# Attention inside a transformer block on eight cores: the probability-times-V matmuls run two groups behind the scores instead of one

## The reference

```python
xn = _layernorm(x, axis=-1)
x = x + attn(xn) + ffn(xn)

# attn
q, k, v = xn@Wq + bq, xn@Wk + bk, xn@Wv + bv
scores = jnp.einsum('bqhk,bshk->bhqs', q, k) * scale
attn = jax.nn.softmax(scores, axis=-1)
ctx = jnp.einsum('bhqs,bshk->bqhk', attn, v)
y = x + jnp.einsum('bqhk,hkd->bqd', ctx, Wo) + bo      # then layernorm, gamma, beta

# ffn: softmax router, top 2 of 8 experts, renormalized
hidden = jax.nn.silu(gate_out) * up_out
expert_out = jnp.einsum('enf,efd->end', hidden, down_w)
```

## Time and profile before

| what | us |
|---|---|
| the three runs | 7039.46, 7514.11, 7524.77 |
| their median | 7514.11 |
| the profiled execution's own time | 7039.46 |
| its span, first to last instruction, slowest core (core 3) | 7037.9 |
| spans of the eight cores | 7002.6 to 7037.9 |
| mean granted TensorE clock of the cores, as a share of 2.4 GHz | 0.788 to 0.791 |

### The profile page before, as it was taken

The page is one execution under the profiler, slowest core; times in us unless marked ns, Lnnn a source line. Parts: engine busy times, 40 slices in busy tenths (PEclk is TensorE's granted clock), DMA queues, the critical chain, the costliest instruction groups (busy, mean ns, idle before and its releaser), DMA issues.

```text
span 7037.9 us, 122186 instructions; the slowest of 8 cores (7002.6 to 7037.9 us)
## 1 busy us (share of the span) xinstructions
PE 5573.7 (79%) x49824; PEld 3157.8 (45%) x49824; DVE 2016.0 (29%) x3908; ACT 2595.2 (37%) x2802; POOL 57.4 (1%) x112
## 2 busy tenths in 40 slices
PE   2577777777777777777777337999999989999999
PEld 1355555555555555555555113444444434444444
DVE  3423232332323233233332563212212211212121
ACT  0266666566666666666666001111111111111111
POOL 0000000000000000000000000000000000000000
PEclk8767566666667666666656668999999999999999
DMA  4022322223131322313222113222222232222222
GB/s 90 31 67 51 80 56 73 74 57 79 49 79 51 80 69 63 79 49 79 63 59 73 57 42 117 72 72 72 72 72 72 72 120 72 72 72 72 72 72 90
DMA packets 125786, 495.52 MB, mean 70 GB/s; under 512 B 13888, under 2 KB 13888, under 8 KB 98112
## 3 DMA queue, kind: packets, MB, share of 16 engines
q1 hardware_dynamic: 87552, 243.31, 10.4%
q0 software_dynamic: 15104, 110.17, 8.8%
q10 hardware_dynamic: 22592, 134.23, 4.9%
HBM read 479.31 MB, written 117.44 MB: 85 GB/s over the span
## 4 chain that ended last, share of the span: by engine, by line
PE 61%; DVE 12%; DMA 11%; ACT 10%; issue 5%; ACTq 0%; DVEq 0%; SPq 0%; POOL 0%; POOLq 0%
PE psA L842 22%; PE psB L886 13%; ACT ptb L529 9%; PE psB L550 9%; DVE ctxa L571 6%; PE psA L514 6%; PE psT L454 4%; DMA pstg<-gate_up 4%; DMA dwb<-wsc 3%; PE psT L479 3%; DMA wsc<-pstg 2%; PE psA L716 1%; DMA pstg<-down 1%; PE psA L316 1%; DVE ktb L464 1%
## 5 line engine op out<-in xcount | busy, mean ns | idle before, releaser
L529 ACT ACTIVATE ptb<-psA,constv 128x1024 bf16<-128x1024 f32 x2048 | 2235.7, 1113 | 1339.2 <-PE psA L514 1173.6
L550 PE MATMUL psB<-vxb,ptb 128*128 128x65 bf16 x16384 | 1143.0, 229 | 892.5 <-ACT ptb L529 481.6
L550 PEld LDWEIGHTS psB<-vxb,ptb 128*128 128x128 bf16 x16384 | 870.6, 119 | 1286.3 <-issue 1259.3
L850 ACT ACTIVATE silb<-psA 128x512 f32<-128x512 f32 x512 | 305.7, 597 | 2374.1 <-PE psA L842 2300.3
L571 DVE TENSOR_TENSOR ctxa<-ctxa,psB 128x455 f32<-128x455 f32 x1488 | 676.9, 511 | 1656.1 <-PE psB L550 1653.8
L514 PE MATMUL psA<-qtb,ktb 64*128 64x128 bf16 x16384 | 1126.5, 282 | 4.7 <-issue 3.8
L842 PE MATMUL psA<-xntf,wgbuf 128*128 128x512 bf16 x4096 | 970.9, 380 | 41.4 <-DVE hidb L854 21.1
L842 PE MATMUL psA<-xntf,wubuf 128*128 128x512 bf16 x4096 | 968.0, 379 | 0.0
L886 PE MATMUL psB<-dwb,hidb 128*128 128x512 bf16 x4096 | 906.6, 385 | 43.5 <-DMA dwb<-wsc 43.5
L854 DVE TENSOR_TENSOR hidb<-silb,psA 128x512 bf16<-128x512 f32 x512 | 352.2, 688 | 1463.0 <-ACT silb L850 1417.7
L514 PEld LDWEIGHTS psA<-qtb,ktb 64*128 64x128 bf16 x16384 | 644.4, 119 | 225.5 <-issue 84.4
(11 more groups left out here) (78 smaller groups left out, 1372.2 us busy)
## 6 DMA issues: line engine op xcount, KB each, us to landing
wsc<-pstg ACTq DMA_DIRECT2D x96, 1024.0 KB, 4.8
pstg<-gate_up POOLq DMA_DIRECT2D x64, 1024.0 KB, 10.4
wgbuf<-wsc SPq DMA_DIRECT2D x256, 256.0 KB, 2.8
wubuf<-wsc SPq DMA_DIRECT2D x256, 256.0 KB, 3.1
dwb<-wsc SPq DMA_DIRECT2D x16, 4096.0 KB, 15.2
xst<-x_batch SPq DMA_DIRECT2D x64, 512.0 KB, 3.4
pstg<-down POOLq DMA_DIRECT2D x32, 1024.0 KB, 10.5
xst<-x_own SPq DMA_DIRECT2D x16, 512.0 KB, 3.5
```

What stands on the lines that cost most here:

```text
L529: e = I("scalar", lambda E, sl=slot, pl=pslot: E.activation(ptb[:, pl * 1024:(pl + 1) * 1024], psA[:, sl * 1024:(sl + 1) * 1024], AF.Exp, ...
L550: sc=sc, par=par: E.matmul(psB[:, co:co + 65], ptb[:, pl * 1024 + pc:pl * 1024 + pc + 128], vxb[:, (par * 2 + sc) * H * 65 + h * 65: (par ...
L850: sl_silu = I("scalar", lambda E, sl=sl: E.activation(silb[:, sl * 512:sl * 512 + TBW], psA[:, sl * 1024:sl * 1024 + TBW], AF.Silu), "tS")
```

## The change

The single pending group becomes a list. A group's PV is issued only when two groups are pending, so that it stands behind the scores of the group two further on. `emit_S`, `emit_exp`, `emit_PV`, the feeder and every other stage are left as they are.

```diff
-            pending = None
+            pending = []
+            def _flush_pv():
+                pgi, pqt, psc, phf = pending.pop(0)
+                pv = emit_PV(pgi, sup, pqt, psc, phf,
+                             first_of_qt=(psc == 0 and phf == 0))
+                if psc == 1 and phf == 1:
+                    prev_ctx_evac_l[0] = emit_ctx_evac(pqt, pv, sup == 0)
+                return pv
             for gli, (qt, sc, hf) in enumerate(groups):
                 smm = emit_S(gidx, sup, qt, sc, hf)
                 attn_last_exp = emit_exp(gidx, smm)
-                if pending is not None:
-                    pgi, pqt, psc, phf = pending
-                    pv = emit_PV(pgi, sup, pqt, psc, phf,
-                                 first_of_qt=(psc == 0 and phf == 0))
-                    if psc == 1 and phf == 1:
-                        prev_ctx_evac_l[0] = emit_ctx_evac(pqt, pv, sup == 0)
-                pending = (gidx, qt, sc, hf)
+                if len(pending) >= 2:
+                    _flush_pv()
+                pending.append((gidx, qt, sc, hf))
                 gidx += 1
...
-            pgi, pqt, psc, phf = pending
-            pv = emit_PV(pgi, sup, pqt, psc, phf, first_of_qt=(psc == 0 and phf == 0))
-            prev_ctx_evac_l[0] = emit_ctx_evac(pqt, pv, sup == 0)
+            while pending:
+                pv = _flush_pv()
```

## The result

Over undisturbed runs the changed kernel takes 1.3411 times as long as before (95% interval 1.3374 to 1.3448). Its fastest run took 9428.73 us, the profiled one 9430.8 us, against 7039.46 us; the median of all 12 is 9627.93 us, that of 14 runs of before 7464.88 us.

The account below looks back on a forecast made before the run. Waits between TensorE and ScalarE in attention were taken to bound the kernel. Groups 5243, turn ends -59 and feeder 676 made attention 5860 us, 2289 more: 9330 us on the 7039.46 us run, range 9000 to 9820.

Parts of the forecast that it names:

- The mechanism: Attention: PV of group g waits for the exponential of g+2, so nothing overlaps, in 62 of 64 PVs a turn.
- the same four steps: Attention group, low clock: PV to scores 0.53, scores to exponential 0.77, exponential 1.11, its end to PV 0.15 us.
- The ends of the turns: Attention, between turns: 5.84 us in place of 7.68, giving back 1.84 x 32 = 59 us.
- The feeder: Attention: TensorE's K, V and transpose work comes on top in full, 21.8 us x 31 turns = 676 us (350 to 998).
- The middle between the clocks: Feeder work per turn: 21.8 us, between 32.2 at the low clock and net 11.3 at the full one.
- full-clock sum: Feeder work per turn at full clock: 7.0 + 7.8 + 1.8 = 16.6 us, net 11.3 after shorter groups.
- rival 1: Clock stays full through attention: 2.17 us a group, attention 4914 us, 8380 in all; chance 0.10.
- The sum: Attention: 5243 - 59 + 676 = 5860 us in place of 3571, 2289 more.
- The clock never rising: Rival 2: low clock in attention, feeder included; attention 6182 us, 9650 in all; chance 0.12.
- The PV that really waits for its own exponential: Rival 3, attention: not slower, TensorE sets the pace, 5.43 us a query tile against 5.87, 6815 in all; chance 0.03.
- ScalarE's wait for weight reads: Attention: 110.3 us in 23 places should go; worth 0 to 110 us, taken as 0.
- PV's wait for exponentials: Sign in attention that the forecast is right: this wait grows from 481.6 us to over 2000 us.

Follow-up runs that it names:

- the first two experiments: First: changed order, each PV waiting for its own exponential's count, 6613.15 us. Second: kernel before with only the late wait, core spans 9479.8 to 9510.3 us.
- the additions by bank: Changed order, each PV waiting for its own exponential, plus `psB` additions made and waited for bank by bank: 6286.66 to 6300.16 us, 0.893 of before.

## Why the prediction was right or wrong

**The mechanism was right.** The overwritten entry makes PV wait for the exponential of two groups on, TensorE and ScalarE take turns, and the first two experiments show it from both sides: repaired, the change gains 6%; put into the old order, the late wait costs the whole loss.

**The size of a group.** 2.56 us predicted at the low clock, 2.55 measured, with the same four steps. What was missed is the second wait of the PV that begins a tile. Its cost was put at nothing: the prediction took that PV to come "2.56 us after it anyway"; it comes at 2.66. This holds for the first PV of every tile but the very first, 511 places, the first of a turn included (idle for 1.52 us at 6062.01 as well, in the rows below), so 56 us.

**The ends of the turns.** Three PVs and three scores stand in a row as foreseen, but from the last PV of a turn that waits too long to the first PV of the next it takes 5.57 us (6056.44 to 6062.01) where 5.84 were predicted, although the 0.11 us of the second wait are in it. The three exponentials between them stand back to back and take 3.14 us, not 3 x 1.11.

```profile
6056.44 1.48 PE L550 MATMUL psB<-vxb,ptb 128*128 128x65 bf16 x24 [1.42 <-ACT ptb L529]
...
6058.62 3.14 ACT L529 ACTIVATE ptb<-psA,constv 128x1024 bf16<-128x1024 f32 x3 [2.32 <-PE psA L514]
...
6062.01 0.60 PE L550 MATMUL psB<-vxb,ptb 128*128 128x65 bf16 x8 [1.52 <-ACT ptb L529]
```

**The feeder.** 21.8 us a turn predicted. Exponentials of a turn with feeder and of the last one, without K and V work (the row's "first and last start"):

```profile
L529 ACT ACTIVATE ptb<-psA,constv x64: 1108/1116/1117, 5871.5 to 6055.2; 128x1024 bf16<-128x1024 f32 x64
...
L529 ACT ACTIVATE ptb<-psA,constv x64: 1108/1116/1117, 6058.6 to 6218.4; 128x1024 bf16<-128x1024 f32 x64
```

The last turn spans 159.8 us from its first exponential to its last. This one takes 183.7 with the feeder, 24 more; over the 31 turns the mean is 22.5, so 697 us against 676. The middle between the clocks was a fair choice, and it does go up and down:

```profile
3137.28 0.60 PE L550 MATMUL psB<-vxb,ptb 128*128 128x65 bf16 x8 [1.42 <-ACT ptb L529]
...
3137.69 3.22 PE L454 MATMUL psT<-xnkb,wkb 128*128 128x256 bf16 x16
...
3140.84 0.40 PE L514 MATMUL psA<-qtb,ktb 64*128 64x128 bf16 x8
...
3144.94 0.60 PE L550 MATMUL psB<-vxb,ptb 128*128 128x65 bf16 x8 [1.42 <-ACT ptb L529]
...
3145.35 3.60 PE L454 MATMUL psT<-xnkb,wkb 128*128 128x256 bf16 x16
...
3148.88 0.61 PE L514 MATMUL psA<-qtb,ktb 64*128 64x128 bf16 x8
```

The first K block begins low and ends high (3.22 us), the next is low throughout (3.60). That the middle came so near is partly luck: at the low clock a K block adds 3.41 us here (3144.94 to 3148.88, less 0.53) and not 3.58, and the prediction's full-clock sum kept the low clock's 0.45 us for a transpose unit, where the run with three extra matmuls shows 0.22 at 2.4 GHz. With the transposes alone put right the middle would have been 21.3 us a turn, and rival 1 some 28 us lower.

**The sum.** Attention 5860 us predicted, 5922 measured: 56 from the second wait and 21 from the feeder, less 15 for a group of 2.55 us rather than 2.56 and for the ends of the turns. The whole profiled execution: 9328 predicted, 9430.8 measured, where 40 of the difference lie behind attention, in stages that were carried over unchanged.

**Where it failed.** The step from the sum to the range. The sum stands on the fastest run, 7039.46 us: 9330, a ratio of 1.325. The time before that was given beside it is a median, 7514.11, and the step "By that spread the same kernel could show 9805" went from the one to the other by adding the 475 us between them to the forecast; this set the top of the range at 9820. A loss that was worked out on one base does not move to another by an addition: the forecast's own ratio makes 9959 us of 7514.11, and the measured one, 1.3411, makes 10077. Both lie above the range. The spread itself did not carry over as 475 us either: the runs of the changed kernel go from 9428.73 to 9959.22, 530 us, while their median stands only 199 above the fastest, and that of the 14 runs before 425. A slowdown is stated safely as a ratio between runs that compare, and a range in microseconds has to say on which base it stands. On the base of its sum, the fastest run, the forecast is some 100 us low, and well inside the range: the second wait, put at nothing, is 56 of them, the stages behind attention are 40 and the feeder 21, less the 15.

**The rivals.** Full clock in attention (8380) did not come by itself; with three extra matmuls in each group the clock in attention was 0.97, attention took 4991 us (4914 in the rival) and the whole 8451, so its working was sound and its condition false. The rule of the Trainium skill named there (TensorE: Matmul & The Clock Gate, HAM oscillation — how this bites in real kernels), long idle gaps as the cause, is borne out neither by the changed kernel, at 0.50 with gaps of 1.4 us, nor by the one extra matmul, at 0.50 with 0.88. The clock never rising (9650) fell with the timeline above. The PV that really waits for its own exponential was forecast at 6815 and measured 6613 when made so: the low clock was assumed for it throughout, and 0.76 was granted on average.

**Minor points.** ScalarE's wait for weight reads (110.3 us before) is gone, as forecast. PV's wait for exponentials reached 2867.9 us ("over 2000").

## What to carry to other kernels

When a pipeline is made deeper, look at the waits and not only at the order: a count kept by slot (group modulo 2) is right only while the consumer runs before the slot's next producer, and a deeper lag silently turns it into a wait for the newest producer, with the same results and in series. Keep the count by item, and check in the waits that the stage that was moved earlier still has something to overlap with. And before deepening, see what waits last: here both the lag with the right wait and the additions by bank paid, together 11%, with the clock that rose along with them.

## What the runs showed of the hardware

In this kernel a matmul that waits on two semaphores starts 0.11 us later than one that waits on a single one, even when the second has long been fulfilled: 2.66 against 2.55 us for a group, in 511 places of the changed kernel, and everywhere when the second wait was put everywhere. At the full clock it is the same 0.11 us: 0.77 against 0.66 us of idle time in the two PVs shown with three extra matmuls.

Exponentials whose scores are there in time start 1.01 us apart although each lasts 1.11 us: six take 6.17 us here, three take 3.14 in the changed kernel, two take 2.12 in the kernel before. One that has to wait for its scores gives its whole 1.11 us to the group.

Giving TensorE useless work can make a kernel faster. Three matmuls of 512 columns in each idle stretch raised the granted clock of the bare groups from 0.50 to 1.00, that of attention as a whole from 0.56 to 0.97, and took 977 us off the changed kernel; one such matmul left the clock of the bare groups at 0.50.
